# Bias of an attention output moved from GpSimd to TensorE, and a power taken of 24 values instead of 4

## The reference, cut to what matters

```
x = x + cross_attention_0(norm(x), ctx, mask)     # q, k, v and output with biases bq, bk, bv, bo
x = x + experts(norm(x))                          # 6 experts of width 128, the best 2 of each row
x = x + cross_attention_1(norm(x), ctx)           # one key and value head
x = x + mlp(norm(x))                              # piecewise linear gelu in fixed point, width 1024
```

## Time and profile before

| | us |
|---|---|
| median of three runs | 809.02 |
| the profiled execution | 809.02 |
| its span, first to last instruction | 806.8 |
| first attention, from the first score to the last one's weighing | about 41 to 231 |
| experts | about 232 to 419 |
| second attention and MLP | about 419 to 807 |

### The profile page before, as it was taken

One profiled execution on the slowest core, in us unless ns is written; L12 is line 12 of the kernel. 1 busy time (PEld: TensorE's weight loads), 2 busy tenths in 40 slices (PEclk: granted clock), 3 DMA queues, 4 the chain that ended last, 5 costly groups with the idle time before them and its releaser, 6 DMA issues.

```text
span 806.8 us, 13562 instructions
## 1 busy us (share of the span) xinstructions
PE 740.1 (92%) x4372; PEld 557.3 (69%) x4372; DVE 654.6 (81%) x1546; ACT 516.2 (64%) x943; POOL 368.3 (46%) x323
## 2 busy tenths in 40 slices
PE   4799999999999999999989999999879899999995
PEld 3566666666567888888864555554568789888895
DVE  7647877777878878888888889889488889899784
ACT  3446565556555446554447776777678797789784
POOL 6373444433212322223213221332377897788785
PEclk9889999999999999999989999999999999999999
DMA  7986634555100000001077657555000000000001
GB/s 226 134 211 122 148 73 78 106 116 109 49 28 1 2 1 7 2 1 53 1 111 98 78 78 129 79 79 72 1 0 1 27 27 2 27 27 28 1 28 52
DMA packets 25101, 48.64 MB, mean 60 GB/s; under 512 B 3686, under 2 KB 7016, under 8 KB 24520
## 3 DMA queue, kind: packets, MB, share of 16 engines
q1 hardware_dynamic: 23366, 46.54, 29.7%
q10 hardware_dynamic: 1666, 1.24, 0.5%
HBM read 12.12 MB, written 4.19 MB: 20 GB/s over the span
## 4 chain that ended last, share of the span: by engine, by line
PE 53%; DVE 19%; issue 8%; ACT 7%; DMA 6%; POOL 5%; DVEq 0%; ACTq 0%; POOLq 0%
PE bank L141 16%; PE bank L649 6%; PE bank L436 6%; PE bank L413 6%; DMA qst<-mt 5%; PE bank L424 5%; PE bank L388 5%; DVE mx L342 3%; PE bank L416 3%; POOL frise L720 2%; DVE fpart L768 2%; DVE x L617 2%; PE bank L391 2%; PE bank L127 2%; DVE fyl L780 2%
## 5 line engine op out<-in xcount | busy, mean ns | idle before, releaser
L316 ACT ACTIVATE pt<-bank 77x512 f32<-77x512 f32 x256 | 140.8, 589 | 80.9 <-PE bank L416 58.4
L342 DVE TENSOR_REDUCE mx<-bank 128x4 f32<-128x308 f32 x256 | 109.1, 471 | 22.8 <-PE bank L391 12.2
L413 PE MATMUL bank<-qst,l_kst 128*77 128x512 f32 (+1 forms) x256 | 102.9, 417 | 15.6 <-DMA qst<-mt 9.7
L720 POOL TENSOR_TENSOR frise<-fg,fg 128x512 f32<-128x512 f32 x64 | 95.7, 1495 | 21.1 <-ACT fg L738 16.6
L388 PE MATMUL bank<-l_kblk,qh 128*128 128x308 f32 x256 | 81.7, 338 | 8.4 <-DVE mx L342 6.0
L284 POOL TENSOR_TENSOR ol<-ot,oh 128x512 fp32r<-128x512 f32 x32 | 41.3, 1290 | 96.5 <-ACT oh L321 53.0
L617 DVE SCALAR_TENSOR_TENSOR x<-bank,eweight,x 128x256 f32<-128x256 f32 x192 | 79.5, 477 | 4.6 <-PE bank L649 4.3
L103 POOL TENSOR_TENSOR rstd<-var,minus_half 128x4 f32<-128x4 f32 x32 | 35.0, 1092 | 103.1 <-DVE var L98 53.9
L413 PEld LDWEIGHTS bank<-qst,l_kst 128*77 128x77 f32 (+1 forms) x256 | 36.5, 146 | 64.8 <-ACT pt L316 24.8
L813 PE MATMUL bank<-fw2h,fyh 128*128 128x256 f32 x256 | 74.0, 289 | 3.8 <-DVE fyl L780 3.8
L388 PEld LDWEIGHTS bank<-l_kblk,qh 128*128 128x128 f32 x256 | 48.1, 192 | 41.8 <-issue 34.0
(11 more groups left out here) (176 smaller groups left out, 2139.5 us busy)
## 6 DMA issues: line engine op xcount, KB each, us to landing
qst<-qh SPq DMA_DIRECT2D x64, 256.0 KB, 6.4
qst<-ql SPq DMA_DIRECT2D x32, 256.0 KB, 8.8
out<-x SPq DMA_DIRECT2D x8, 512.0 KB, 2.6
qst<-ml SPq DMA_DIRECT2D x8, 480.0 KB
x<-in_x SPq DMA_DIRECT2D x3, 1024.0 KB, 12.4
weights<-in_mlp_w SPq DMA_DIRECT2D x2, 1024.0 KB, 5.7
mraw<-in_mask SPq DMA_DIRECT2D x8, 154.0 KB
x<-in_x SPq DMA_DIRECT2D x2, 512.0 KB, 5.6
```

The costliest lines, as they stand in the source:

```text
L316: self.nc.scalar.activation(self.pt[0:T, i // 4 % 2, i % 4, :], self.bank_of(G, i)[0:T, :], ACT.Exp).then_inc(self.probs, 1)
L342: self.nc.vector.reduce_max(out, banks[u % len(banks)][:, 0:4 * T].rearrange("q (p par t) -> q p par t", p=2, par=2), AX.X).then_inc(self. ...
L413: last = self.nc.tensor.matmul(out, layer.kst[rows, layer.stack(c * HC + 2 * k + par), b * T:(b + 1) * T], self.qst[rows, self.slot(G), c ...
L720: self.nc.gpsimd.tensor_tensor(self.rise[:, k % 2, :], self.g1[:, k % self.R, :], self.g0[:, k % self.R, :], ALU.subtract).then_inc(self.r ...
```

## The change

The addition of `bo` by GpSimd is gone, and with it `add_bias`, the load of `bo` and VectorE's wait for `biased`. Instead `bias` holds the high part of `bo` on partition 0 and its low part on partition 32 (zeros elsewhere), twice side by side, and `ones` is a 128 x 128 tile of ones; in `output` of the first attention one matmul `ones` x `bias` of 512 columns starts the bank, and the twelve others add to it. `bo` comes in with the row of `bv`. GpSimd clears `bias` and fills `ones` before its 16 key products; VectorE makes the two parts after the layer norm of block 1. In the router, the power is now taken of all 24 values of `below`; the two instructions that made `gap` are gone, and `share` is a masked product, a sum, a reciprocal and a product.

```diff
         self.cols = place.at("cols", m["cols"], [P, 2, C], F32)
-        self.bo = place.at("bo", m["bo"], [P, D], F32)
+        self.bias = place.at("bias", m["bias"], [P, 2, D], F32R)
+        self.ones = place.at("ones", m["ones"], [P, P], F32R)
         self.mraw, self.mh = place.at("mraw", m["mraw"], [T, N], F32), place.at("mh", m["mh"], [P, N], F32R)
...
-    def add_bias(self, pool, G):
-        pool.wait_ge(self.norm.normed, G + 1)
-        for k in range(2):
-            start = G * NT + 2 * k
-            tiles = self.norm.x[:, start:start + 2, :]
-            self.nc.gpsimd.tensor_tensor(tiles, tiles, self.bo[:].unsqueeze(1).to_broadcast([P, 2, D]), ALU.add).then_inc(self.biased, 1)
-            pool.wait_ge(self.biased, 2 * G + k + 1)
-
...
         dve.wait_ge(self.out_done, 2 * G + k + 1)
-        if G < BLOCKS:
-            dve.wait_ge(self.biased, 2 * G + k + 1)
         start = G % BLOCKS * NT + 2 * k
...
         pe.wait_ge(self.ol_ready, C * (G + 1))
+        if layer.masked:
+            nc.tensor.matmul(self.W[k][:, :], self.ones[:, :], self.bias[:].rearrange("r k d -> r (k d)"), start=True, stop=False)
         for t in range(2):
             tile = slice((2 * k + t) * P, (2 * k + t + 1) * P)
             for c in range(C):
                 for a, w in ((self.oh, layer.woh), (self.oh, layer.wol), (self.ol, layer.woh)):
                     last = nc.tensor.matmul(self.W[k][:, t * D:(t + 1) * D], a[:, c, tile], w[:, c, :],
-                                            start=(c == 0 and a is self.oh and w is layer.woh),
-                                            stop=(c == C - 1 and a is self.ol))
+                                            start=(not layer.masked and c == 0 and a is self.oh and w is layer.woh),
+                                            stop=(c == C - 1 and a is self.ol and (not layer.masked or t == 1)))
         last.then_inc(self.out_done, 1)
...
         pool.wait_ge(self.below_ready, g + 1)
-        self.nc.gpsimd.tensor_tensor(self.ex[:], self.euler[:], self.gap[:], ALU.pow).then_inc(self.ex_ready, 1)
+        self.nc.gpsimd.tensor_tensor(self.ex[:], self.euler[:], self.below[:], ALU.pow).then_inc(self.ex_ready, 1)
         pool.wait_ge(self.ex_ready, g + 1)
...
         self.put(nc.vector.reduce_sum(self.rank[:], self.above[:], AX.X))
-        self.put(nc.vector.tensor_tensor(self.below[:], self.logit[:], self.top[:].to_broadcast([P, NT, E]), ALU.subtract))
-        dve.wait_ge(self.router_chain, self.chain)
-        self.put(nc.vector.scalar_tensor_tensor(self.second[:], self.rank[:], 1.0, self.below[:], ALU.is_equal, ALU.mult))
-        dve.wait_ge(self.router_chain, self.chain)
         need(dve, self.ex_ready, g)
-        nc.vector.reduce_sum(self.gap[:], self.second[:], AX.X).then_inc(self.below_ready, 1)
+        nc.vector.tensor_tensor(self.below[:], self.logit[:], self.top[:].to_broadcast([P, NT, E]),
+                                ALU.subtract).then_inc(self.below_ready, 1)
     def share(self, dve, g):
         nc = self.nc
         dve.wait_ge(self.ex_ready, g + 1)
         dve.wait_ge(self.router_chain, self.chain)
-        self.put(nc.vector.scalar_tensor_tensor(self.second[:], self.rank[:], 1.0, self.ex[:].to_broadcast([P, NT, E]), ALU.is_equal,
-                                                ALU.mult))
-        self.put(nc.vector.tensor_scalar(self.total[:], self.ex[:], 1.0, None, ALU.add))
+        self.put(nc.vector.scalar_tensor_tensor(self.exs[:], self.rank[:], 2.0, self.ex[:], ALU.is_lt, ALU.mult))
         dve.wait_ge(self.router_chain, self.chain)
-        self.put(nc.vector.scalar_tensor_tensor(self.exs[:], self.rank[:], 0.0, self.second[:], ALU.is_equal, ALU.add))
+        self.put(nc.vector.reduce_sum(self.total[:], self.exs[:], AX.X))
+        dve.wait_ge(self.router_chain, self.chain)
         self.put(nc.vector.reciprocal(self.rtotal[:], self.total[:]))
...
                     if G == 2:
-                        sp.wait_ge(v_done, 2)
+                        sp.wait_ge(bias_ready, 1)
                         sp.wait_ge(id5_ready, 1)
...
                 norm.invert(pool, 1)
+                nc.gpsimd.memset(att.bias[:].bitcast(F32), 0.0).then_inc(cleared, 1)
+                pool.wait_ge(cleared, 5)
+                nc.gpsimd.memset(att.ones[:].bitcast(F32), 1.0).then_inc(cleared, 1)
+                pool.wait_ge(cleared, 6)
                 pool.wait_ge(kt_ready, 1)
...
                             att.rest_quotient(pool, G - 1, c)
-                    if G == 0:
-                        pool.wait_ge(att.bo_in, 16)
-                        for k in range(2):
-                            att.add_bias(pool, k)
-                    if G + 2 < BLOCKS:
-                        att.add_bias(pool, G + 2)
                     if G == 3:
+                        pool.wait_ge(bias_ready, 1)
                         pool.wait_ge(id5_ready, 1)
...
                 act.dma_start(msel[:], d["minus"]).then_inc(vo_in, 16)
-                act.dma_start(att.bo[:], d["bo"].to_broadcast([P, D])).then_inc(att.bo_in, 16)
                 act.wait_ge(q_in, 32)
...
                     norm.rest(dve, 1, c, att.W[c], att.xh, att.xl)
+                dve.wait_ge(cleared, 6)
+                dve.wait_ge(vo_in, 64)
+                for k in range(2):
+                    nc.vector.tensor_copy(att.bias[0:1, k, :], rows[:, 1, :]).then_inc(bias_chain, 1)
+                dve.wait_ge(bias_chain, 2)
+                for k in range(2):
+                    last = nc.vector.tensor_tensor(att.bias[32:33, k, :], rows[:, 1, :], att.bias[0:1, k, :].bitcast(F32), ALU.subtract)
+                last.then_inc(bias_ready, 1)
                 for G in range(BLOCKS):
...
                                         pe.wait_ge(wol_ready, 1)
+                                        pe.wait_ge(bias_ready, 1)
+                                        pe.wait_ge(cleared, 6)
                                     if n < BLOCKS:
```

More of the change, by code:

```diff
@@ L211, in __init__ @@
         self.added = sem("added")
-        self.bo_in = sem("bo_in")
-        self.biased = sem("biased")
         self.STACK_INC = 16 * 3
@@ L471, in __init__ @@
         self.tempc, self.clip, self.half = small("tempc", [P, 1], F32), small("clip", [P, 1], F32), small("half", [P, 1], F32)
-        self.euler = small("euler", [P, NT, 1], F32)
+        self.euler = small("euler", [P, NT, E], F32)
         self.logit, self.above = small("logit", [P, NT, E], F32), small("above", [P, NT, E, E], F32)
@@ L475, in __init__ @@
         self.below = small("below", [P, NT, E], F32)
-        self.gap, self.ex = small("gap", [P, NT, 1], F32), small("ex", [P, NT, 1], F32)
-        self.exs, self.second = small("exs", [P, NT, E], F32), small("second", [P, NT, E], F32)
+        self.ex, self.exs = small("ex", [P, NT, E], F32), small("exs", [P, NT, E], F32)
         self.total, self.rtotal = small("total", [P, NT, 1], F32), small("rtotal", [P, NT, 1], F32)
@@ L827, in memory_map @@
           "wol": z + 64000, "kt": m["oh"], "kh": m["oh"] + 2464, "kl": m["oh"] + 4928}
-    m.update({"mraw": z + 51712, "mh": z + 53760, "ml": z + 55808, "mm": z + 57856, "bo": z + 66048,
+    m.update({"mraw": z + 51712, "mh": z + 53760, "ml": z + 55808, "mm": z + 57856, "bias": z + 66048, "ones": z + 68096,
               "id5": z + 68608, "klowf": z + 70176, "rows": z + 70816, "ones_row": z + 72864, "id5f": z + 73184})
@@ L862, in build @@
         id5f = place.at("id5f", m["id5f"], [P, 5 * T], F32)
-        rows = place.at("rows", m["rows"], [1, D], F32)
+        rows = place.at("rows", m["rows"], [1, 2, D], F32)
         ones_row = place.at("ones_row", m["ones_row"], [1, T], F32)
@@ L883, in build @@
         id5_ready, wqh_ready, wql_ready = sem("id5_ready"), sem("wqh_ready"), sem("wql_ready")
-        woh_ready, wol_ready = sem("woh_ready"), sem("wol_ready")
+        woh_ready, wol_ready, bias_chain, bias_ready = sem("woh_ready"), sem("wol_ready"), sem("bias_chain"), sem("bias_ready")
         k_done, v_done, v_ready = sem("k_done"), sem("v_done"), sem("v_ready")
@@ L1506, in _ @@
                         nc.tensor.matmul(bank, ctx[:, k, b * T:(b + 1) * T], wv0[:, k, :], start=(k == 0), stop=False)
-                    last = nc.tensor.matmul(bank, ones_row[:, :], rows[:], start=False, stop=True)
+                    last = nc.tensor.matmul(bank, ones_row[:, :], rows[:, 0, :], start=False, stop=True)
                     if b % 2:
@@ L1738 @@
         "cols": arr(np.stack([column(L0_xattn_bq), column(L0_xattn_bk)], axis=1)),
-        "rows": arr(L0_xattn_bv).reshape(1, D), "bo": arr(L0_xattn_bo).reshape(1, D),
+        "rows": arr(np.stack([np.asarray(L0_xattn_bv), np.asarray(L0_xattn_bo)])[None]),
         "wq0": arr(np.asarray(L0_xattn_Wq).T[:, feature]), "wk0": arr(np.asarray(L0_xattn_Wk).T[:, feature]),
```

## The result

The changed kernel took 817.07 us (median of four runs, 815.70 to 820.88) against 809.12 for the kernel before on the same chip: a ratio of 1.0107, with an interval of 1.0069 to 1.0145. It is slower, as forecast, but by 8 us and not by 22.5. The profiled execution took 817.71 us with a span of 815.9; before these were 809.02 and 806.8.

A forecast was written before the change was run, and what follows sets the result against it. The prediction took TensorE's nearly unbroken chain in the first attention and experts as the bound; 3.7 (bias) + 17.2 (seven groups) + 1.6 (group 0) = 22.5 us on 809.02 gave 831.5 us, range 813 to 845.

The forecast's parts named there:

- 1.32 + 20 x 0.22 = 5.7 us: Experts' router: GpSimd's power of 24 values, from 1.32 us for 4 values and 0.22 us for each further value.
- 17.2: Experts: seven groups each 2.45 us longer because share and the add wait for the power, +17.2 us.
- +1.6: Experts, group 0: share starts at 243.7 against 242.1 because of the longer power, +1.6 us.
- (c): Rival, experts: the long power keeps VectorE from subtracting, 1.1 us more a group, 839 us; chance 0.03.
- A group grows by the power's time less 3.25 us: Experts: general rule for how much a group lengthens, with 3.25 us of the power's time taken off.
- not below -0.3: Experts: two router instructions less save at most 0.3 us a group, -2.1 us if nothing takes their place.
- bias matmuls, 0.23 us each: First attention's output: 16 added matmuls on TensorE's chain, 0.23 us each, +3.7 us.
- GpSimd's freed 2.6 us a block: First attention: dropping GpSimd's bias additions frees 2.6 us a block, but nothing starts earlier, 0 us.
- I take 0: Setup: GpSimd's clearing and VectorE's four instructions are covered, 0 us; 0.8 us if the cover failed.
- (a): Rival, experts: the power costs nearly the same for 24 values, 810.6 us; chance 0.11.
- (b): Rival, experts: TensorE's clock falls to 1.2 GHz after idling some 2.5 us a group, 839 us; chance 0.16.
- (d): Rival, MLP: a shifted MLP may miss all six half-clock places, -7 us, 804 us with a cheap power; chance 0.06.

The follow-up runs named there:

- e8: GpSimd's powers and subtraction without layers, alone and beside one VectorE instruction: beside a subtraction of two SBUF tiles, power of 4 values 1.31 us for 1.01.
- e2: The kernel before with the change's bias part alone (bias matmuls, new setup, old router): 808.24 us, ratio 1.0063.
- e7: The changed kernel with the power of two of the four tiles, 12 values a partition, constant weights for the others: 811.47 us, ratio 1.0062.
- e5: The changed kernel with GpSimd's two setup clearings moved to the start of its stream: 814.97 us, ratio 1.0120.
- e1: The kernel before with the router part alone (power of 24 values, new share), bias left on GpSimd: 811.78 us, ratio 1.0112.

## Why the prediction was right in direction and wrong in size

**The step that failed is the price of a value in the power.** The forecast put "1.32 + 20 x 0.22 = 5.7 us". Measured: 1.01 + 20 x 0.158 = 4.16 alone, and 4.70 beside VectorE's subtraction. Two wrong readings lie in it. The 1.32 us held 0.31 of waiting (e8) that doesn't grow with the values, and the forecast made it a part of the price a value. And of the power's 0.81 us over a product, 0.18 are fixed. The two terms of the forecast are measured from one `share` to the next, against e2, which has the same bias matmuls. The term "17.2" for seven groups became 7.6 us: 1.31 to 1.39 in five, 0.76 in group 4, 0.07 in group 2. By the forecast's own rule a power of 4.70 us makes 10.2 of the 17.2 (7 x 1.45); the other 2.6 are the longer cover of group 2 and the shorter power of group 4. The term "+1.6" for group 0 became 0.3: its `share` starts 35.02 us after block 7's maxima (246.28 and 211.26) and 34.74 in e2.

The row that told of it was in the trace before: the power of 128 x 4 had a maximum of 1550 ns on the same shape, and each time VectorE's subtraction had started just before it. Under rival (c) the forecast says of the shared ports that "the trace doesn't show it here"; it looked at the earlier trace rows alone, where the power came first.

**The mechanism held.** Power, wait of VectorE, `share`, add, wait of TensorE, with everything behind it moving along: the page, the chain and the twelve-value run show each link. "A group grows by the power's time less 3.25 us" would give 1.45 us at 4.70; 1.33 to 1.38 was measured where nothing else lies. It failed where the cover was longer (group 2: 0.04), which no step had looked at: the forecast took group 6 for all seven.

**The router's saving, "not below -0.3", is nothing.** The chain's piece before `share` is the low part of expert 2 and not the router (e7). The 0.17 us that TensorE waited before expert 5's output are gone in e7 and come back as 0.16 to 0.20 before expert 1's in most groups. In the forecast `share` was put behind the power, though in the earlier trace rows 1.67 us lie between the power's end at 369.14 and `share` at 370.81, and that gap should have been asked about.

**The bias matmuls, 0.23 us each, are right:** 0.48 a block in five blocks, and in e2 alone the same. That GpSimd's freed 2.6 us a block bring nothing also held.

**The setup, "I take 0",** was some 0.6 us in the profiled pair and 1.0 over all profiles. The cover was reckoned at TensorE's first use of the mask copy. By e5's rows the one that failed is on the queue, of which the forecast said that "the block waits for its maxima, which come later still". They come later, but in the same queue behind the stacks; that the stacks were still landing then fits the times from issue to landing, and one profile with early clearings is all that tests it. VectorE's four instructions took 1.9 us there (38.37 to 40.26) and not "1.6 us at most", for the wait on GpSimd's products that e8 explains; nothing waited for them.

**Rivals.** (a), the cheap power, is false. The Trainium skill (GPSIMD Engine Reference, section Performance versus the Vector engine) gives a two-input tensor_tensor about 2.6 cycles an element. Where the operation is a power the trace does not follow it: 0.158 us a value, against 0.0017 for a product ((0.234 - 0.201)/20). (b), half clock in the experts, is not in the profile after, though TensorE stands 1.50 us in group 5, and is in e1's once, behind 1.94 us. (c) is false: the low part of expert 2 took its 0.69 us within the power. (d) happened in part: -3.4 us in the profiled execution. The forecast let it decide only beside a cheap power, but it is a term of its own: it comes and goes in both kernels.

**The sum.** By the profiled pair: 1.0 (start, bias and setup) + 2.4 + 8.9 + 0.2 - 3.4 = 9.1 us of span, and 8.7 of time. By the forecast's terms that is 3.8 for the bias (3.7), 0.6 for the setup (0), 7.9 for the power (17.2 + 1.6), 0.2 in the second attention (0) and -3.4 in the MLP (0). So 10.9 of the 13.4 us too much are the power, and the rest is mainly the clock in the MLP. The 817 us lie near the low end of the range, which was put at a power of 3.5 us and has no term for the MLP.

## What to carry to other kernels

Two durations of the same operation on the same shape are a price and a wait until shown otherwise: before a difference is put down to the data, look at what the other engines did at that moment. Before an operation's time is multiplied up, ask for a second size; where none is in the trace, both ends of the range belong in the forecast, and here the true slope, 0.158 us a value, lay below both slopes, 0.20 and 0.28, that two rows had seemed to give. And the work that sets a waiting instruction is found by what ended just before it, not by what it depends on: `share` depended on the power and waited for something else.

## What the runs showed of the hardware

- GpSimd's power costs 0.38 us and 0.158 for each value of a partition (4 to 48 values), for all bases and exponents tried; a product of the same shapes costs 0.20 to 0.28 us.
- GpSimd's power, and its subtraction, wait at their start for a VectorE operation on two SBUF tiles that is under way. The wait is what is left of that operation less 0.14 us: 0.31 us with 0.45 left (e8), 0.53 with 0.68 left (experts).
- The other way round it depends on GpSimd's operation. VectorE, started 0.4 us or more into a running power, isn't held up (0.69 us as ever). Beside GpSimd's key products, VectorE's subtraction of 256 values on one partition took 677 to 781 ns for 412: it waited until the product ended, less 0.14 us.
- An idle time of some 2 us in TensorE, repeated in every group of the MLP, is followed by a fall to 1.2 GHz in some executions and not in others. Seven dummy matmuls of 512 columns in it (1.75 us) keep 2.4 GHz, make the kernel before 0.4% faster (0.1 to 0.7%) and halve the spread of its runs. No kernel measured has a lower median.
